# Attention and mixture-of-experts layer on one core: where sixteen dense blocks stand around the expert slots, and how the experts' down weights are split

## The reference

```
x = x + xattn(layernorm(x), ctx)                  # rows "x1"
h = layernorm(x)                                  # rows "z"
scores = softmax(h @ gate.T); top 2 of 8 experts per token
y  = sum over the 2 picks of  w * (silu(h @ Wg_e.T) * (h @ Wu_e.T)) @ Wd_e.T      # F = 352
y += (silu(h @ Sg.T) * (h @ Su.T)) @ Sd.T         # "shared" part, 704 wide, every token
out = x + y
```

## Time and profile before

| | |
|---|---|
| median of three timed runs | 1583.47 us (1582.27 to 1590.14) |
| the profiled execution's own time | 1578.52 us |
| its span in the trace | 1576.6 us |
| PE busy | 1417.7 us, 90% |
| PEld / DVE / ACT / POOL busy | 68% / 58% / 41% / 31% |
| mean DMA rate over the span | 143 GB/s |
| mean granted TensorE clock | 0.957 |

### The profile page before, as it was taken

How to read it: one execution, slowest core, us unless ns; L and a number is a source line. 1 busy time by engine, 2 the same in 40 slices (tenths; PEclk the granted TensorE clock), 3 DMA queues, 4 the chain that set the end, 5 groups by cost and what they waited for, 6 DMA issues and landing times.

```text
span 1576.6 us, 33371 instructions
## 1 busy us (share of the span) xinstructions
PE 1417.7 (90%) x10371; PEld 1072.0 (68%) x10388; DVE 912.8 (58%) x1984; ACT 648.7 (41%) x1500; POOL 496.6 (31%) x607
## 2 busy tenths in 40 slices
PE   5489999999999998788899966999999999999685
PEld 4488888888888886656576643666666666666453
DVE  6588888888888887658444534232232222322565
ACT  4255555666666664422133433333333333332111
POOL 4244444443444443105562000111111111112664
PEclk9699999999999998989999978999999999999888
DMA  5546766666667768382445134222222222223897
GB/s 181 112 119 169 172 171 172 170 174 182 194 191 182 175 147 265 101 337 57 77 51 101 53 129 137 67 84 83 81 85 81 80 86 80 85 81 118 302 323 258
DMA packets 265808, 225.20 MB, mean 143 GB/s; under 512 B 183430, under 2 KB 191694, under 8 KB 265759
## 3 DMA queue, kind: packets, MB, share of 16 engines
q1 hardware_dynamic: 247832, 180.46, 40.8%
q0 software_dynamic: 12880, 35.47, 7.6%
q10 hardware_dynamic: 5046, 8.66, 1.6%
HBM read 130.35 MB, written 69.01 MB: 126 GB/s over the span
## 4 chain that ended last, share of the span: by engine, by line
PE 71%; DVE 8%; DMA 8%; ACT 4%; issue 4%; SPq 2%; POOL 1%; another core or an unknown queue 0%; ACTq 0%; DVEq 0%; POOLq 0%
PE psum_b L707 38%; PE psum_a L707 27%; PE psum_b L1016 2%; DMA wdn_in<-in_wdn_t 2%; SPq L471 2%; DMA wgu_in<-expert_rows,pos_ix 2%; PE psum_a L804 2%; PE psum_b L1038 1%; ACT spread_t L1086 1%; DMA base_rows<-base 1%; DVE d_m L1696 1%; DMA base<-x_rows 1%; DMA wgu_in<-base_rows 1%; PE psum_b L733 1%; DVE gate_act L1671 1%
## 5 line engine op out<-in xcount | busy, mean ns | idle before, releaser
L707 PE MATMUL psum_a<-wgu,zg_t 128*128 x1704 | 268.0, 314 | 2.1 <-DVE zg_t L1809 1.7
L1932 POOL TENSOR_TENSOR spread<-pr,own 128x512 f32<-128x512 f32 x128 | 136.7, 1099 | 318.0 <-DVE pr L1448 306.7
L707 PEld LDWEIGHTS psum_a<-wgu,zg_t 128*128 128x128 f16 x1704 | 167.0, 98 | 89.9 <-issue 10.4
L2006 POOL DMA_INDIRECT zg<-z_rows,gather_ix x71 | 67.2, 946 | 503.1 <-DVE gather_ix L1805 495.9
L707 PE MATMUL psum_b<-wsdn,sh_t 128*128 128x512 f16 (+1 forms) x576 | 148.9, 412 | 54.8 <-DVE sh_t L1677 54.6
L707 PE MATMUL psum_a<-zt_in,wsgu 128*128 128x256 f16 x1536 | 172.3, 274 | 6.6 <-DMA base<-x_rows 4.6
L707 PEld LDWEIGHTS psum_a<-zt_in,wsgu 128*128 128x128 f16 x1536 | 149.8, 98 | 31.4 <-issue 6.3
L1814 DVE SCALAR_TENSOR_TENSOR silu<-psum_a,w_scale,silu 128x352 f32<-128x352 f32 x71 | 41.4, 584 | 194.1 <-ACT silu L1287 194.1
L707 PEld LDWEIGHTS psum_b<-wsdn,sh_t 128*128 128x128 f16 (+1 forms) x576 | 55.8, 103 | 141.8 <-DVE sh_t L1677 65.5
L707 PE MATMUL psum_b<-wdn,act_t 128*128 (+1 forms) x639 | 149.6, 379 | 1.6 <-DVE act_t L1821 1.6
L1287 ACT ACTIVATE silu<-psum_a,w_scale 128x352 f32<-128x352 f32 x71 | 39.3, 553 | 202.9 <-PE psum_a L707 202.9
(11 more groups left out here) (244 smaller groups left out, 2491.9 us busy)
## 6 DMA issues: line engine op xcount, KB each, us to landing
expert_rows<-y_sb SPq DMA_DIRECT2D x71, 256.0 KB, 2.0
k_st<-k_parts SPq DMA_DIRECT2D x192, 64.0 KB, 2.1
q_st<-q_parts SPq DMA_DIRECT2D x192, 64.0 KB, 2.1
wgu_in<-in_wgu_t SPq DMA_DIRECT2D x8, 1408.0 KB, 18.0
x_sb<-in_x SPq DMA_DIRECT2D x16, 512.0 KB, 3.4
cx_in<-in_ctx_t SPq DMA_DIRECT2D x16, 512.0 KB, 7.0
x_res<-in_x SPq DMA_DIRECT2D x16, 512.0 KB, 5.3
value_rows<-heads SPq DMA_DIRECT2D x16, 512.0 KB, 7.0
```

The lines of the kernel that those rows point to most:

```text
L707: return nc.tensor.matmul(o, l, r, start=start, stop=stop)
L1932: G.tensor_tensor(spread[:, u * UG:(u + 1) * UG, :].rearrange("p r (g t) -> p r g t", t=GT), pr[:, s, u * UG:(u + 1) * UG, :].unsqueeze(3) ...
L2006: pool.indirect_dma_start(out=zg[:, b, :], out_offset=None, in_=z_d[:, :], in_offset=bass.IndirectOffsetOnAxis(ap=gather_ix[:, b:b + 1], a ...
```

## The change

- `SHARED_FIRST` goes from 12 to 10: blocks 10 and 11 run behind the slots, so that six dense blocks stand there; `TAIL_TILES = [3, 5, 5, 5, 6, 6]` spreads 30 combine steps over them, and two are left for the end as before.
- `CONVERT_FROM` goes from 6 to 5: the gate/up weights are split in blocks 5 to 8.
- The down weights are loaded by three DMAs, one per row chunk, into a raw area `wdn_in` of 26 places of 2 KB per partition that overlaps `zg` and the split `wdn`, shifted by two places. The pieces are split from the last place to the first: 16 in block 4 and 8 in block 9, and the result overwrites raw places already used (`down_high(n)` waits until `down_low(n-2)` is done). Two of the loads are issued after `r_pos`, before block 2's store; the third in SP's program before block 8's store, once the gate/up weights are split.
- The list of slot tokens is turned inside block 9 (`ids_out` behind chunk 3), and the first two gathers can start there; `zg` has a place of its own.
- The base rows of blocks 14 and 15 are neither stored nor loaded again: `combine` reads them from `base`.
- Loops over dense blocks ahead of the slots are written out.
- The scratch of the routing moves into the raw area.

```diff
-CONVERT_FROM = 6
+CONVERT_FROM = 5
+DOWN_ORDER = [2, 0, 1]
-SHARED_FIRST = 12
-TAIL_TILES = [6, 8, 8, 8]
+SHARED_FIRST = 10
+TAIL_TILES = [3, 5, 5, 5, 6, 6]
...
+        wdn_in = sb("wdn_in", [P, len(DOWN_ORDER) * E + 2, D], F32, wdn_place)
+        wdn_place.close()
+        zg = sb("zg", [P, 2, D], F32, two)
+        wdn = sb("wdn", [P, len(DOWN_ORDER), E * 2 * D], F16, two)
...
+        DOWN_EARLY, DOWN_LATE = CONVERT_FROM - 1, SHARED_FIRST - 1
+        PIECES_AT = {DOWN_EARLY: [3, 3, 3, 1, 3, 3], DOWN_LATE: [0, 4, 4, 0, 0, 0]}
...
+            def stage_down(place):
+                f0, fn = F_CH[DOWN_ORDER[place]]
+                sp.dma_start(wdn_in[0:fn, place * E:(place + 1) * E, :], wdn_t[f0:f0 + fn]).then_inc(wd_staged[place], 16)
+
+            for i in range(SHARED_FIRST):
+                if i == 2:
+                    sp.wait_ge(r_pos, 1)
+                    stage_down(2)
+                    stage_down(1)
+                if i == SHARED_FIRST - 2:
+                    sp.wait_ge(w_low16, 1 + 2 * E)
+                    stage_down(0)
                 store_base(i, i % 2, i // 2, True)
...
-                store_base(i, i % 2, i // 2, i + 2 < NB)
+                if i + 2 < NB:
+                    store_base(i, i % 2, i // 2, True)
...
+            gate_up(last_one, 1, range(4))
+            pe.wait_ge(sh_out, last_one * SH_STEPS)
+            pe.wait_ge(ids_float, 1)
+            nc.tensor.transpose(psum_b[3][:, 0:SLOTS], id_rows[:, :], ident[0:SLOTS, 0:SLOTS]).then_inc(ids_turned, 1)
+            gate_up(last_one, 1, range(4, 6))
+            pe.wait_ge(g_ix, 1)
+            down(last_one, 1)
...
             def down_high(n):
+                whole_values, hi, _, scale, staged = piece(n)
+                act.wait_ge(staged, 16)
+                if n >= 2:
+                    act.wait_ge(wd_low, n - 1)
+                nc.scalar.activation(hi, whole_values, ACT.Copy, scale=scale).then_inc(wd_high, 1)
...
-                        if n < SUB * i:
+                        if n < min(SUB * i, NT - 2 * SUB):
...
+            def ids_out():
+                dve.wait_ge(ids_turned, 1)
+                link(V.tensor_copy(ids_col[:, :], psum_b[3][:, 0:SLOTS]))
+                index_out(0, 0, 0)
+                index_out(1, 1, 0)
...
             def combine(n, b, k):
-                dve.wait_ge(cb_loaded[b], k * 16 + 16)
+                i = n // SUB
+                if i < NB - 2:
+                    dve.wait_ge(cb_loaded[b], k * 16 + 16)
+                    tile_base = comb[2][:, b, :]
+                else:
+                    dve.wait_ge(sh_out, (i + 1) * SH_STEPS)
+                    tile_base = base[:, i % 2, n % SUB, :]
```

More of the change, by code:

```diff
@@ L402, in stat_no, with pieces_at, piece @@
             return i * (2 * SUB) + (2 * SUB + s + 1 - SUB * missing)
-        PIECES = [(f, e) for f in range(len(F_CH)) for e in range(E)]
-        def pieces_at(step):
-            return range(step * 2, min(step * 2 + 2, len(PIECES)))
+        PIECES = len(DOWN_ORDER) * E
+        DOWN_EARLY, DOWN_LATE = CONVERT_FROM - 1, SHARED_FIRST - 1
+        PIECES_AT = {DOWN_EARLY: [3, 3, 3, 1, 3, 3], DOWN_LATE: [0, 4, 4, 0, 0, 0]}
+        def pieces_at(i, f):
+            first = sum(PIECES_AT[i][:f]) + (sum(PIECES_AT[DOWN_EARLY]) if i == DOWN_LATE else 0)
+            return range(first, first + PIECES_AT[i][f])
+        def piece(n):
+            slot = PIECES - 1 - n
+            place, e = slot // E, slot % E
+            fn = F_CH[DOWN_ORDER[place]][1]
+            return (wdn_in[0:fn, slot, :], wdn[0:fn, place, e * 2 * D:e * 2 * D + D], wdn[0:fn, place, e * 2 * D + D:(e + 1) * 2 * D],
+                    wd_scale[0:fn, 2:3], wd_staged[place])
         wsdn_loaded = sem("wsdn_loaded")
@@ L421, in build @@
         w_rep_ready, w_rep_turned = sem("w_rep_ready"), sem("w_rep_turned")
[L422 removed]
+        wd_staged = [sem(f"wd_staged{n}") for n in range(len(DOWN_ORDER))]
         wd_scaled, wd_high, wd_low = sem("wd_scaled"), sem("wd_high"), sem("wd_low")
@@ L654, in _ @@
             sp.dma_start(token_d.rearrange("(j p) o -> j (p o)", p=P), zero_id[:, :]).then_inc(zero_stored, 16)
[L655 to L671, removed]
-                        if n + 2 < len(PIECES):
-                            stage_down(n + 2)
+            def stage_down(place):
[9 more added lines that the diff above has]
+                    stage_down(0)
                 store_base(i, i % 2, i // 2, True)
@@ L1263, in down_high @@
             def down_high(n):
-                f, e = PIECES[n]
-                fn = F_CH[f][1]
-                act.wait_ge(wd_staged[n % 2], 16 * (n // 2 + 1))
-                nc.scalar.activation(wdn[0:fn, f, e * 2 * D:e * 2 * D + D], wdn_in[0:fn, n % 2, :], ACT.Copy, scale=wd_scale[0:fn, 2:3]).then_inc(wd_high, 1)
-            for first, end, converts in ((2, CONVERT_FROM, False), (CONVERT_FROM, CONVERT_FROM + E // 2, True)):
-                with act.Fori(first // 2, end // 2) as k:
-                    for b in range(2):
-                        gates(k * 2 + b, lambda f: weights_high16(k * 2 + b, f) if converts and f < 4 else None)
+                whole_values, hi, _, scale, staged = piece(n)
[3 more added lines that the diff above has]
+                nc.scalar.activation(hi, whole_values, ACT.Copy, scale=scale).then_inc(wd_high, 1)
+            for i in range(2, DOWN_EARLY):
+                gates(i, lambda f: None)
+            act.wait_ge(wd_scaled, 1)
+            gates(DOWN_EARLY, lambda f: [down_high(n) for n in pieces_at(DOWN_EARLY, f)])
+            for i in range(CONVERT_FROM, CONVERT_FROM + E // 2):
+                gates(i, lambda f: weights_high16(i, f) if f < 4 else None)
             act.wait_ge(w_low16, 1 + 2 * E)
-            act.wait_ge(wd_scaled, 1)
-            for i in range(CONVERT_FROM + E // 2, SHARED_FIRST):
-                gates(i, lambda f: [down_high(n) for n in pieces_at((i - CONVERT_FROM - E // 2) * len(FS_CH) + f)])
+            gates(DOWN_LATE, lambda f: [down_high(n) for n in pieces_at(DOWN_LATE, f)])
             a_bank, d_bank = psum_b[1], psum_b[2]
```

56 lines of the change are left out of this document (22 added, 34 removed).

## The result

The changed kernel takes 1512.35 us (median of 4 runs, 1504.44 to 1513.93) against 1582.87 us for the kernel before on the same chip: a ratio of 0.9537, 95% interval 0.9491 to 0.9584. Two later comparisons gave 0.9547 [0.9506, 0.9588] and 0.9537 [0.9516, 0.9559], 72 and 74 us less by the medians. Predicted were 1518 us and -65. The profiled execution took 1513.9 us (span 1512.2) against 1578.5 us before, that is -64.6 on the executions' own times.

What follows compares the result with a forecast made beforehand. PE's chain of waits bounds it, with gaps in blocks 10 and 11 and a DMA-bound tail. Head -78.2, slots -1.0, tail +13.9 give -65.3 us: 1513 for the profiled execution, 1518 for the median, range 1505 to 1544.

Steps and rivals of the forecast that it cites:

- Staging: 0 us: Head: the first two raw down-weight loads, issued at 717.7 us, land at 728 at 402 GB/s and cost nothing.
- the 18 us of room behind 728: Head: slack after the two staging loads' forecast landing at 728 us, given as a reason for staging costing 0.
- the rule weighed: Staging: DMA engines take turns between queue rows, a packet at a time, so big loads beside the scatter cost nothing: 1518.
- Block 4: +2.5: Head: block 4 with 16 down-weight pieces takes 2.5 us over 22.57, nearest to DVE's sum; ends 0 and +12.
- The strict alternation (+12): Block 4: ACT and DVE alternate strictly on the pieces, block about 12 us longer, 1530; chance inside the main case's 0.61.
- Blocks 5 to 8: 92.9: Head: these blocks carry what blocks 6 to 9 carried and take the same 92.9 us, one stretched to 24.7.
- Block 9 23.5, hand-over: Head's end: block 9 takes 22.7 plus 0.8 for `g_ix`; list and gather inside it, first slot product at 906.2 us.
- The slots: -1: Slots: the first product group starts with less delay, giving 1 us back; ends 0 and 2.
- Tail: 148.2: Block 10 to the span's end: blocks 141.7 us plus 6.5 behind PE's end, 13.9 more than before.
- the rival of PE's pace: Tail blocks at 22.7 us, block 4 not longer, no late arrival: 6 to 9 us less, 1510; chance 0.14.
- the 3 us named as a sign of being wrong: Tail: the forecast is wrong if blocks show DVE waiting for expert rows by more than 3 us each.
- price for the DMAs: Tail blocks 11 to 13: five combine steps move 6.8 MB, 20.9 us at 327 GB/s, under PE's 22.6.

Runs made afterwards that it cites:

- the last experiment: The changed kernel as it is, run again unchanged as a measure for other runs on its chip: 1506.27 us (1505.02 to 1510.93), ratio 0.9537.
- experiment 8: The changed kernel with the first two raw down-weight loads issued behind block 4's load, at 746 us in place of 717.7: 1529.53 us in one run.
- experiment 9: The changed kernel with the list's turn and the first two gathers put back behind block 9: 1513.02 us beside the changed kernel's 1506.27.
- experiments 5, 6: 5: the changed kernel itself, 1509.05 us; 6: the changed kernel with blocks 10 and 11 back ahead of the slots, same chip, 1536.74 us.
- 2: The kernel before with only the base rows of blocks 14 and 15 read from their buffer: 1586.52 us against 1595.66, ratio 0.9945.

## Why the prediction was right, and where it was off

- *What bounds it.* PE's chain, as read from the earlier trace rows. The three places named (blocks 10 and 11, the hand-over, the tail) gave what there was to gain.
- *Staging: 0 us.* Right in what it costs: no wait of ACT for `wdn_in` in the head, where it was 30.2 us. Wrong in how fast it is: 28.2 us to the second load's landing in the last experiment's profile, not 10.4 for both, so that of the 18 us of room behind 728 nothing was left at 746. No reason that was given carries it. The 1.3 us ahead of the scatter did not spare the loads, and the "205 and 307 GB/s" of the earlier trace rows are two slices of 0.2 us each. What carried it, the lead of 47 us to the first piece's use, stands in no term (experiment 8). On the rule weighed (the Trainium skill, "DMA: Bandwidth & Descriptors", section "Queues, rings and completion order"): if turns between queue rows let the big loads through almost unhindered, as the prediction reads it, experiment 8 with 39.5 us for 4.19 MB does not agree, nor do the 28.2 us of the changed kernel.
- *Block 4: +2.5.* Right: +2.3 without the scatter (24.7), and 24.8 in the one profile of the changed kernel in which block 4 was not disturbed. Of it 1.39 us are the late hidden value of the forecast; 0.48 are the wait for the scale's signal, which it did not have. The strict alternation (+12) didn't come; its case of 1530 counted the 2.5 us twice, and should have been 1527.5.
- *Blocks 5 to 8: 92.9.* 89.6 to 93.9. Written out they run at 22.4, 0.3 below a looped block, which the prediction didn't have; what is above 89.6 is gone without the scatter. It is not always a stop without a name: in the last experiment's profile block 7's input load came 2.8 us late, and the granted clock was 0.93 behind that gap:

```profile
833.18 12.16 PE L716 MATMUL psum_a<-zt_in,wsgu 128*128 128x256 f16 x96 [2.78 <-DMA base<-x_rows]
```

- *Block 9 23.5, hand-over.* 22.6 to 22.7: the +0.8 for PE's wait for `g_ix` wasn't needed. The third load took 8.9 us, not 4, within the 12.5 that were there. The hand-over's 6 us are shown by experiment 9.
- *The slots: -1.* Not found: +0.9, and -0.8 in the other profile; no sign either way.
- *Tail: 148.2.* 143.3 to 144.0. The forecast of 23.5 for blocks 11 to 13 was 0.3 to 1.0 too long; only block 14 with its six steps is above PE's pace (24.3, forecast 25.0). Here the rival of PE's pace was nearer, and its whole time of 1510 us is nearer to the measured 1512 than 1518 is, though block 4 was longer, which it denies. DVE's waits for expert rows are down to 4.1 us in all from 22.1; the longest, 3.3 us in block 10, is above the 3 us named as a sign of being wrong, but cost PE nothing. Its price for the DMAs was right: 306 GB/s for 23.2 us are 7.1 MB, forecast 6.8, and they fit. Behind PE's end 6.5 us, as forecast (1505.7 to 1512.2).
- *What was missed.* Block 3 at 28.2 and block 4 at 27.0 in the first profile, 32.4 for block 4 in the second, 39.8 with twelve ahead: gaps with no cause in the profile, and late loads, beside the scatter. The kernel before had the like (a block of 24.7 in the earlier trace rows), and I took it over as one stretched block. It costs 5.5 us in the median and makes a spread of 6 to 11 us; no term stood for it. It was covered, since the tail was 4.2 us shorter than forecast and blocks 5 to 9 some 3.
- *The sum.* -65.3 on the executions' own times, -64.6 measured. That these agree to 1 us is luck: the head gained 3.3 us less than forecast, the slots 1.9 less, and the tail cost 4.2 less. The median was carried over with the 5 us by which the profiled execution before lay under its median. After, the profiled execution was the slowest of four; by the medians of the three comparisons the change is worth 70.5 to 74.0 us, so the typical gain is 5 to 9 us above the forecast, the tail's 4 and the blocks' 3 among them.

Shares of the gain, each measured by itself: the two blocks 27.7 us (experiments 5, 6), the hand-over 6.8 (9), the base from its buffer some 4 to 9 (2, measured on the kernel before, interval 3 to 14). The new staging took 41.0 + 32.4 - 22.4 - 22.7 = 28.3 us from blocks 10 and 11, by the earlier trace rows and the windows of experiment 6, less block 4's 2.3: 26. It was not undone by itself, so what in it is the early load and what the order of the pieces is not shown. Together this is 65 to 70 of the 72 us; the rest is within what the runs of one kernel differ by.

## What to carry to other kernels

When a stage is bound by DMAs, the idle time of the bounding engine of the other stages is a place to put work: count it first (33 us here), then move as much as fits, and look at the clock too, since long gaps can cost twice. A load's price is set by when it is issued: 47 us ahead of its first use it cost nothing, though the scatter held it to 28 us; issued 28 us later, it cost 18 us. Before a wait is read as a stop, look whether a run without the suspect has it too under another name. Waits in program order make even one more combine step in the wrong block cost 4 us, so a table of steps per block deserves its own look at which rows can have landed by then.

## What the runs showed of the chip that was not expected

- Beside 64 indirect DMAs that write 4-byte words, PE's matmuls come singly, with gaps of 0.2 to 2.5 us for which the profile shows nothing missing ("issue"), at other places in each run: 2 us of gaps in one block, or a block of 39.8 us, or of 56.6. Without the scatter this is gone, and the runs agree within 2.2 us in place of 10.7. That single packets of the instruction queue took about 3 us there is a reading of the trace; that they are the cause is argued, not shown.
- Large loads beside the same scatter land late: 28.2 us in place of 12.2 for the second of two of 2.1 MB, and 39.5 us when issued 28 us into it.
- Where PE had long gaps, the granted clock was lower and the work itself longer: block 4 with 32.4 us (gaps of 1.0 to 1.7 us with single matmuls between) had PE busy 26.3 us at a granted clock of 0.84, with 24.7 us it was 22.8 at 1.00. Block 3 with 28.2 us, with gaps of 0.2 to 1.7 us, kept 1.00. So a stop of a few us can cost more than itself.
- Dense blocks with four pieces of gate/up weights take 22.4 us written out and 22.7 in a loop.
